# Node rows of a partition side by side: storing zu in another order and mapping the source list to it

## What is computed

```python
# layer 0 (4 heads of 16)
ZU = einsum('nd,kdr->knr', x, U);  zs, zd = ZU[:, src], ZU[:, dst]
alpha = segment_softmax((zs * zd).sum(-1) / 4, dst)
agg = segment_sum(alpha[..., None] * zs, dst)
ssa = einsum('k,knr,kdr->nd', softmax(head_w), agg, U)
Z_half = 0.5 * x + 0.5 * ssa
L0 = relu(Z_half + 0.5 * ((Z_half - (Z_half @ Dmat.T) @ Dmat) @ Dmat) - 0.05)
x = layernorm(x + L0)
# layer 1
agg = segment_sum(x[src], dst) / max(count, 1)
x = layernorm(x + relu(agg @ W_l.T + b_l + x @ W_r.T) + x)
```

## Time and profile before

| what | us |
|---|---|
| median of 3 runs (4514.98 to 4522.93) | 4522.0 |
| the profiled execution's own time | 4529.45 |
| its span, first to last instruction | 4527.6 |
| GpSimd busy in it (3493 instructions) | 3300.4 (73%) |
| VectorE busy | 2281.5 (50%) |
| TensorE, ScalarE busy | 931.8, 785.6 |
| edges of layer 0, GpSimd's part | 165.5 to 2205.5 |
| node stage of layer 0 | 2236 to 2396 |
| edges of layer 1, GpSimd's part | 2404.4 to 4340.7 |

### The profile page before, as it was taken

The page is one execution under the profiler, slowest core; times in us unless marked ns, Lnnn a source line. Parts: engine busy times, 40 slices in busy tenths (PEclk is TensorE's granted clock), DMA queues, the critical chain, the costliest instruction groups (busy, mean ns, idle before and its releaser), DMA issues. The chain is left out here.

```text
span 4527.6 us, 46280 instructions
## 1 busy us (share of the span) xinstructions
PE 931.8 (21%) x3091; PEld 613.9 (14%) x3091; DVE 2281.5 (50%) x9502; ACT 785.6 (17%) x1441; POOL 3300.4 (73%) x3493
## 2 busy tenths in 40 slices
PE   7301112111112000000293221122222221112027
PEld 7301101001001000000151110011111111001025
DVE  2107656666566666566473444344344344334348
ACT  2001101001001000000052222222222222222125
POOL 6677777777777777777565777777777777777755
PEclk6555555556556555555585555555555555555569
DMA  9803243333333322224284656666666666666769
GB/s 349 316 27 123 87 132 97 97 122 97 98 122 96 109 81 89 81 81 138 70 269 161 223 206 213 241 240 241 240 228 214 229 213 207 219 240 232 256 219 322
DMA packets 347584, 795.44 MB, mean 176 GB/s; under 512 B 94902, under 2 KB 235419, under 8 KB 317796
## 3 DMA queue, kind: packets, MB, share of 16 engines
q1 hardware_dynamic: 164706, 380.87, 23.6%
q0 software_dynamic: 137712, 276.64, 20.2%
q10 hardware_dynamic: 44818, 135.00, 7.7%
HBM read 420.40 MB, written 371.83 MB: 175 GB/s over the span
## 5 line engine op out<-in xcount | busy, mean ns | idle before, releaser
L575 POOL DMA_INDIRECT sb_big<-x,sb_idx x1549 | 1464.6, 946 | 502.8 <-issue 471.8
L575 POOL DMA_INDIRECT sb_big<-zu_rows,sb_idx x1531 | 1445.2, 944 | 478.4 <-issue 466.3
L1466 DVE SCALAR_TENSOR_TENSOR ps_V<-ps_V,sb_keepc,sb_big 128x256 f32<-128x256 f32 x1518 | 747.6, 493 | 132.7 <-ACT sb_big L1053 79.4
L1053 ACT COPY sb_big<-ps_V 128x1024 f32<-128x1024 f32 (+1 forms) x414 | 399.5, 966 | 1288.2 <-DVE ps_V L1466 1285.3
L762 PE MATMUL ps_T<-sb_ident,sb_xg 128*128 128x128 f32 x392 | 114.6, 390 | 2402.6 <-ACT sb_tileT L898 1225.0
L1466 DVE SCALAR_TENSOR_TENSOR ps_V<-ps_E,sb_keepc,sb_big 128x256 f32<-128x256 f32 x46 | 22.7, 492 | 1020.4 <-DMA sb_big<-x,sb_idx 981.0
L762 PEld LDWEIGHTS ps_T<-sb_ident,sb_xg 128*128 128x128 f32 x392 | 72.1, 201 | 2461.0 <-ACT sb_tileT L898 1236.2
L1272 DVE TENSOR_TENSOR_SCAN sb_big<-ps_E,sb_big 128x34 f32<-128x34 f32 x2944 | 355.3, 203 | 1.6
L1220 DVE TENSOR_TENSOR_SCAN ps_V<-ps_V,sb_big 128x34 f32<-128x34 f32 x2944 | 354.6, 206 | 0.0
L1229 DVE TENSOR_TENSOR sb_big<-ps_V,sb_big 128x2176 f32<-128x2176 f32 x46 | 111.4, 2421 | 351.3 <-DMA sb_big<-zu_rows,sb_idx 351.3
L575 POOL DMA_INDIRECT sb_hn<-rows,sb_nidx x196 | 189.5, 967 | 75.3 <-issue 53.6
(11 more groups left out here) (240 smaller groups left out, 1845.7 us busy)
## 6 DMA issues: line engine op xcount, KB each, us to landing
rows<-sb_big SPq DMA_DIRECT2D x46, 3072.0 KB, 10.7
rows<-sb_big SPq DMA_DIRECT2D x46, 1280.0 KB, 13.8
rows<-sb_big ACTq DMA_DIRECT2D x46, 1224.0 KB
z_at_start<-sb_big ACTq DMA_DIRECT2D x46, 1088.0 KB, 8.7
sb_big<-z_at_start SPq DMA_DIRECT2D x46, 1088.0 KB, 5.2
sb_zx<-zu_rows SPq DMA_DIRECT2D x2816, 0.2 KB
sb_big<-x SPq DMA_DIRECT2D x1920, 1.0 KB
sb_xg<-in_x_dram SPq DMA_DIRECT2D x36, 768.0 KB, 6.2
```

The lines of the kernel that those rows point to most:

```text
L575: pool.indirect_dma_start(to, None, table, bass.IndirectOffsetOnAxis(ap=index.bitcast(U32), axis=0), **more).then_inc(done, 16)
L1053: act.copy(slot1[s][:, cols, :], V0[:, first_word:first_word + width].rearrange("p (c f) -> p c f", f=D)).then_inc(col_copied, 1)
L1466: dve.scalar_tensor_tensor(out=sums_at(j), in0=before, scalar=keepc[:, j:j + 1], in1=slot1[s][:, j, :], op0=ALU.mult, op1=ALU.add).then_in ...
```

## The change

`zu_rows` gets another row order: within a group, the seven nodes of a partition stand side by side (row = 896 g + 7 p + b in place of 896 g + 128 b + p), so that each partition stores 1792 B in one piece. All other tables stay. Everything that reads `zu_rows` needs the new row numbers: VectorE maps `src_i` in place, and the one column for the carry row, with shifts and multiplications (six operations each, `rows_placed`); ScalarE waits for it before the first index copies. The offsets for layer 1 (`row_bytes[1]`) are made before the mapping. Between the layers VectorE maps `src_i` back in nine operations, with `normed` as working space, ahead of the scaling of group 0. The mapping uses the space of zs[0], so the zeros move to a piece of their own, half as long, which each fill reads twice. And GpSimd's queue changes its order: the gathers of chunk 1 now stand directly behind those of chunk 0, ahead of the scatters and the carry row.

```diff
@@ -79,9 +79,12 @@
     RB = 16
     U8 = mybir.dt.uint8
     NZ = 4
+    NTH, NTH_BITS = 147, 10
+    RTH, RTH_BITS = 9363, 16
     NX = 4
     assert FP * FQ == NF and FQ * FW <= C * F and CA % GC == 0 and NGC % 2 == 1 and C % GC == 2 and NG * GB == NB and NG % NX == 2 and NCH % 4 == 2 and NCH % S1 == 1 and NCH % 2 == 0 and NG < NCH // S1 and 0 < ELAST <= COLS and NF * FW == E
-    assert E <= EP and D == 2 * P
+    assert E <= EP and D == 2 * P and all(b * NTH >> NTH_BITS == b // GB for b in range(NB))
+    assert all(r * RTH >> RTH_BITS == r // GB for r in range(GN)) and GN * RTH < 1 << 24
 
     zu_rows = nc.dram_tensor("zu_rows", (NP, F), F32, kind="Internal").ap()
     z_at_start = nc.dram_tensor("z_at_start", (EP + NP, F), F32, kind="Internal").ap()
@@ -119,8 +122,8 @@
 
         regA = in_big(4 * C * F)
+        block_i = regA[:, 0:COLS].bitcast(I32)
         dst_i = regA[:, 2 * C * F:2 * C * F + COLS + 2].bitcast(I32)
-        zero = regA[:, C * F:2 * C * F]
         zs = [regA[:, s * C * F:(s + 1) * C * F].rearrange("p (c f) -> p c f", f=F) for s in range(2)]
         zd = [regA[:, (2 + s) * C * F:(3 + s) * C * F].rearrange("p (c f) -> p c f", f=F) for s in range(2)]
         zu = in_big(NB * F).rearrange("p (b f) -> p b f", f=F)
@@ -136,6 +139,7 @@
         Wraw = in_big(2 * KD * D).rearrange("p (w k n) -> p w k n", w=2, k=KD)
         Dm = in_big(KD * D).rearrange("p (k n) -> p k n", k=KD)
         DtD = in_big(KD * D).rearrange("p (k n) -> p k n", k=KD)
+        zero = in_big(C * F // 2)
 
         at_node = [0]
 
@@ -217,6 +221,8 @@
         zx_act = sb("zx_act", [P, F])
         nidx = [sb(f"nidx{s}", [P, GB], I32) for s in range(2)]
         zcar0 = sb("zcar0", [P, F])
+        zcar_i = sb("zcar_i", [P, 1], I32)
+        zcar_b = sb("zcar_b", [P, 1], I32)
         scar = sb("scar", [P, F + H])
         logit = sb("logit", [P, H, C])
         keepc = sb("keepc", [P, C])
@@ -271,7 +277,7 @@
         rows_counted = sem("rows_counted"); row_step = sem("row_step"); rows_known = sem("rows_known")
         found_rows = sems("found_rows", 2)
         first_known = sem("first_known"); next_made = sem("next_made"); nodes_known = sem("nodes_known"); z_scattered = sem("z_scattered")
-        zcar_loaded = sem("zcar_loaded")
+        zcar_loaded = sem("zcar_loaded"); rows_placed = sem("rows_placed")
         w_pe = sem("w_pe"); w_dve = sem("w_dve"); w_exp = sem("w_exp")
         idx_ready = sems("idx_ready", 2); zs_gathered = sems("zs_gathered", 2)
         zd_loaded = sems("zd_loaded", 2); zd_used = sems("zd_used", 2)
@@ -327,6 +333,10 @@
             return blocks(dram, g, 0, GB)
 
+        def side_by_side(dram, g):
+            return dram[bass.ds(g * GN, GN), :].rearrange("(p b) f -> p b f", p=P)
+
+
         def node_groups_of(engine, body):
 
             for u in range(NX):
@@ -388,7 +398,7 @@
 
             def store_zu(i, s):
                 sp.wait_ge(zu_copied, 2 * i + s + 1)
-                sp.dma_start(node_group(zu_rows, 2 * i + s), zu[:, bass.ds((2 * i + s) * GB, GB), :]
+                sp.dma_start(side_by_side(zu_rows, 2 * i + s), zu[:, bass.ds((2 * i + s) * GB, GB), :]
                              ).then_inc(zu_stored, 16)
 
             load_x(0, 0)
@@ -593,6 +603,7 @@
 
             pool.wait_ge(zu_stored, 16 * NG)
             gather_zs(0, 0, 0, 0)
+            gather_zs(0, 1, 0, 0)
 
             pool.wait_ge(nodes_known, 1)
             for q in range(NZ):
@@ -601,8 +612,8 @@
                 pool.indirect_dma_start(z_at_start, bass.IndirectOffsetOnAxis(ap=scat_i[:, b:b + 1].bitcast(U32), axis=0),
                                         zu[:, b, :], None).then_inc(z_scattered, 16)
 
-            gather(zcar0[:, :], zu_rows, dst_i[:, 1:2], zcar_loaded)
-            gather_zs(0, 1, 0, 0)
+            pool.wait_ge(rows_placed, 2)
+            gather(zcar0[:, :], zu_rows, zcar_i[:, 0:1], zcar_loaded)
 
             def later_rounds(i, pair, odd):
                 if isinstance(i, int) and i == 0:
@@ -863,7 +874,8 @@
             def fill(k, q):
 
                 wait(act, zero_filled[q], 16 * k)
-                act.dma_start(z_flat[:, bass.ds((NZ * k + q) * C * F, C * F)], zero).then_inc(zero_filled[q], 16)
+                act.dma_start(z_flat[:, bass.ds((NZ * k + q) * C * F, C * F)].rearrange("p (a f) -> p a f", a=2),
+                              zero.unsqueeze(1).broadcast_to([P, 2, C * F // 2])).then_inc(zero_filled[q], 16)
 
             act.wait_ge(zero_set, 1)
 
@@ -882,7 +894,7 @@
                              B[s][:, 0:GB * F].rearrange("p (b f) -> p b f", f=F)).then_inc(zu_copied, 1)
 
             rounds(act, NG // 2, project)
-            act.wait_ge(edges_loaded, 16 * 6)
+            act.wait_ge(rows_placed, 2)
             for s in range(2):
                 act.copy(idx[s][:, :], src_i[:, s * C:(s + 1) * C]).then_inc(idx_ready[s], 1)
             for k in range(NG // 2, -(-NCH // NZ)):
@@ -1111,6 +1123,23 @@
             dve.wait_ge(edge_ends, 32)
             dve.tensor_tensor(keep[:, :], dst_i[:, 1:COLS + 1], dst_i[:, 0:COLS], ALU.is_equal)
             dve.tensor_copy(ends, col_i)
+
+            for k, step, width in ((1, S1, D),):
+                last_cols = src_i[:, 0:NCH // step * step * C].rearrange("p (i c) -> p i c", c=step * C)[:, :, 2 * C - 1]
+                dve.tensor_scalar(row_bytes[k][:, :], last_cols, float(4 * width), None, ALU.mult
+                                  ).then_inc(rows_scaled, 1)
+            dve.wait_ge(rows_scaled, 1)
+
+            for row, blk, node_of in ((src_i[:, 0:COLS], block_i, src_i[:, 0:COLS]),
+                                      (zcar_i[:, :], zcar_b[:, :], dst_i[:, 1:2])):
+                done(dve.tensor_scalar(blk, node_of, P.bit_length() - 1, None, ALU.logical_shift_right))
+                done(dve.tensor_scalar(row, node_of, P - 1, None, ALU.bitwise_and))
+                done(dve.scalar_tensor_tensor(out=row, in0=row, scalar=float(GB), in1=blk, op0=ALU.mult, op1=ALU.add))
+                done(dve.tensor_scalar(blk, blk, float(NTH), None, ALU.mult))
+                done(dve.tensor_scalar(blk, blk, NTH_BITS, None, ALU.logical_shift_right))
+                dve.scalar_tensor_tensor(out=row, in0=blk, scalar=float(GN - GB), in1=row, op0=ALU.mult, op1=ALU.add
+                                         ).then_inc(rows_placed, 1)
+            dve.wait_ge(rows_placed, 2)
             done(dve.tensor_tensor(same, dst_i[:, 1:COLS + 1], dst_i[:, 2:COLS + 2], ALU.is_equal))
             done(dve.scalar_tensor_tensor(out=ends, in0=same, scalar=OUT_OF_RANGE, in1=ends, op0=ALU.mult,
                                           op1=ALU.add))
@@ -1189,7 +1218,7 @@
                                              ).then_inc(w_dve, 1)
 
-            for k, step, width in ((0, 2, F), (1, S1, D)):
+            for k, step, width in ((0, 2, F),):
                 last_cols = src_i[:, 0:NCH // step * step * C].rearrange("p (i c) -> p i c", c=step * C)[:, :, 2 * C - 1]
                 dve.tensor_scalar(row_bytes[k][:, :], last_cols, float(4 * width), None, ALU.mult
                                   ).then_inc(rows_scaled, 1)
@@ -1427,6 +1456,19 @@
 
             first_indices(0)
+
+
+            nodes_of = src_i[:, 0:COLS]
+            high, low = (n.rearrange("p b f -> p (b f)")[:, 0:COLS].bitcast(I32) for n in normed)
+            done(dve.tensor_scalar(high, nodes_of, P.bit_length() - 1, None, ALU.logical_shift_right))
+            done(dve.tensor_scalar(high, high, float(NTH), None, ALU.mult))
+            done(dve.tensor_scalar(high, high, NTH_BITS, None, ALU.logical_shift_right))
+            done(dve.tensor_scalar(high, high, float(GN), None, ALU.mult))
+            done(dve.scalar_tensor_tensor(out=nodes_of, in0=high, scalar=-1.0, in1=nodes_of, op0=ALU.mult, op1=ALU.add))
+            done(dve.tensor_scalar(low, nodes_of, float(RTH), None, ALU.mult))
+            done(dve.tensor_scalar(low, low, RTH_BITS, None, ALU.logical_shift_right))
+            done(dve.scalar_tensor_tensor(out=nodes_of, in0=nodes_of, scalar=float(P), in1=high, op0=ALU.mult, op1=ALU.add))
+            done(dve.scalar_tensor_tensor(out=nodes_of, in0=low, scalar=float(1 - GN), in1=nodes_of, op0=ALU.mult, op1=ALU.add))
             scale(0, 0, 0)
 
             def node_step(t, u):
```

## The result

| what | before | after |
|---|---|---|
| median of six runs each, us (lowest to highest) | 4522.81 (4514.98 to 4530.56) | 4548.26 (4545.36 to 4557.42) |
| the profiled execution's own time, us | 4529.45 | 4545.36 |
| GpSimd's first gather of zu rows | 165.51 | 156.63 |
| first scatter | 208.20 | 242.08 |
| first gather of chunk 2 | 378.84 | 405.06 |

The kernel became slower: ratio 1.006, 95% interval 1.0047 to 1.0073. The forecast was 4551 us, slower, 4540 to 4561; it held.

A forecast was written before the change was run, and what follows sets the result against it. GpSimd's gathers of zu rows, 1.249 us each, were taken to set the pace. Stall +33.7, front -7.5 and middle +3 sum to +29.2 us: 4551 against the median, range 4540 to 4561.

The forecast's parts named there:

- (a): GpSimd's queue order: nothing left to cover the chain to ScalarE's index copy, a stall of 33.7 us ahead of chunk 2.
- (b): Store of zu side by side: lands sooner, gaining between nothing and 11.55 us of GpSimd's wait of 11.86.
- (c): Map ahead on VectorE: holds up GpSimd's lookups by 4 us, range 0 to 6; front with store gains 7.5.
- Rival 1: The stall stands but VectorE does not hold GpSimd up: +22 us, 4544; chance 0.15.
- the three slow lookups agree: GpSimd's first lookups, 2.43, 2.11 and 1.49 us in place of 0.94, taken to support VectorE's two-port modes excluding GpSimd.
- the scatter at 208.20 without a wait: Front: taken to show all fills of zeros landed by then; the new order asks for them some 35 us later.
- (d): Map back between the layers: gathers beside it start about 4 us late, partly absorbed; +3 us, range 0 to 5.
- rival 4: Node stage: the granted clock falls elsewhere, sparing 13 us (4538) or adding as many; chance 0.07.
- Rival 2: Store: pieces stay 256 B or land no sooner, GpSimd starts at 165.5 as before: +36.7 us, 4559; chance 0.08.
- Rival 3: Later rounds: SyncE becomes the pace-maker; a round 1 us longer costs 8 us, 4559; chance 0.07.
- Rival 5: Gathers from the new table are cheaper on GpSimd; 40 ns less each gives 61 us, 4490; chance 0.03.

The follow-up runs named there:

- order alone: Kernel before with chunk 1's gathers moved ahead and a separate, half-long piece of zeros; old table, no map: 4547.67 us, ratio 1.0056.
- finer fills, whole memset: Kernel before whose fills read the first half of the piece of zeros twice, memset left whole: 4515.59 us in one run.
- finer fills: Kernel before with a half-long piece of zeros that each fill reads twice, memset half as long: 4521.73 us against 4526.96, ratio 0.9993.
- 6 ahead, old table: Kernel before with 6 of chunk 1's gathers ahead of the scatters, 28 behind the carry row, separate half-long zeros, no maps: 4516.77 us, ratio 0.9977.
- order undone: Changed kernel with chunk 1's 34 gathers behind the carry row again: 4525.81 us against 4521.06, ratio 1.0008.
- 6 ahead: Changed kernel with 6 of chunk 1's 34 gathers ahead of the scatters, 28 behind the carry row: 4518.52 us against 4521.06, ratio 0.9991.
- after, again: Changed kernel profiled once more, unchanged: 4551.6 us.
- 20 ahead: Changed kernel with 20 of chunk 1's 34 gathers ahead of the scatters, 14 behind the carry row: 4546.88 us.
- before, again: Kernel before profiled once more, unchanged: 4551.47 us.
- store alone: Kernel before with only the store side by side, list unmapped so wrong rows are gathered: 4517.06 us in one run, beside 4516.06.
- both maps: Changed kernel without the mapping ahead and back, so wrong rows are gathered, with the same amount of work: 4543.87 us, ratio 1.0047.

## Why the prediction was right

*(a) The stall.* This term was right, with its mechanism: predicted 33.7 us, measured 405.06 - 368.96 = 36.10 from the carry row's start to the next gather, less its own 1.27, so 34.8 (35.12 idle, with the usual 0.3 in it; 34.86, 35.15 and 35.16 idle in three other profiles). From the carry row's start to the end of ScalarE's copy it took 34.96 us before and 35.22 after (368.96 to 403.96 + 0.22); another 0.88 us passed until the gather began, of which the forecast had counted nothing. That it isn't given back is shown by the end of the edges, +26.2 us, where chunk 2 already stood. The lead of ScalarE's copy in the even chunks fell to 6.8 us at its least (6 predicted).

*(b) and (c), the front.* The sum was right (−7.5 predicted, −8.88 measured), and both parts are seen. The wait of 11.86 us fell to the usual 0.30 and the map ahead lengthened the lookups by 4.4 us (4 predicted), which makes −7.2. The other −1.7 is nothing that the prediction counted: the first lookup began at 26.51 in place of 28.23. In profiles of kernels that have at most one part of the change it begins anywhere from 26.32 to 28.40, so this much may be luck. GpSimd's and then VectorE's timeline of the changed kernel, to be held against the earlier trace rows:

```profile
26.51 2.42 POOL L585 DMA_INDIRECT sb_hn<-in_dst_dram,sb_frow_i  x1 [19.47 <-DVE sb_frow_i L1120]
29.24 1.80 POOL L585 DMA_INDIRECT sb_hn<-in_dst_dram,sb_frow_i  x1 [0.30 <-issue]
31.35 2.53 POOL L585 DMA_INDIRECT sb_hn<-in_dst_dram,sb_frow_i  x1 [0.30 <-issue]
34.18 1.40 POOL L585 DMA_INDIRECT sb_hn<-in_dst_dram,sb_frow_i  x1 [0.30 <-issue]
35.88 1.52 POOL L585 DMA_INDIRECT sb_hn<-in_dst_dram,sb_frow_i  x1 [0.31 <-issue]
```

```profile
29.95 0.97 DVE L1136 TENSOR_SCALAR sb_src_i<-sb_src_i 128x1564 int32<-128x1564 int32 x1
30.96 1.79 DVE L1137 SCALAR_TENSOR_TENSOR sb_src_i<-sb_src_i,sb_big 128x1564 int32<-128x1564 int32 x1
32.78 0.97 DVE L1138 TENSOR_SCALAR sb_big<-sb_big 128x1564 int32<-128x1564 int32 x1
33.79 0.97 DVE L1139 TENSOR_SCALAR sb_big<-sb_big 128x1564 int32<-128x1564 int32 x1
34.80 1.79 DVE L1140 SCALAR_TENSOR_TENSOR sb_src_i<-sb_big,sb_src_i 128x1564 int32<-128x1564 int32 x1
```

Rival 1, that VectorE does not hold GpSimd up, is thereby out: without the maps the second to fifth lookup take 0.97, 1.36, 1.52 and 0.94 us in place of 1.80, 2.53, 1.40 and 1.52, the two longer ones beside the wide operations that stay, and the lookups as a whole are 5.3 us shorter (from 26.33 to 150.86). A lookup that began at 29.24 ended at 31.04, 0.12 us after the tensor_scalar of line 1136; one that began at 31.35 ended at 33.88, 0.13 after that of line 1138. The prediction's reading of the earlier trace rows, that each of the first three lookups ended 0.8 us after a wide operation, holds for the second and third; the first ended 0.13 us after the cast (30.66 against 30.53). Of the three only that one has a cast beside it; the other two stand beside operations with two operands alone, so that the prediction's "the three slow lookups agree", said of two-port modes, holds for one of them. They are taken up at the end.

What the prediction did not see is what the gain of the front depends on. It priced the store and the order as terms that add up. They don't: undone, the order leaves chunk 2 where it was, although the first gather still starts 9 us earlier. It read the scatter at 208.20 without a wait as fills that were out of the way; they had landed within some 2 us before it. The windows of before would have told (us, busy and count of PE, PEld, DVE, ACT, POOL; clock, DMA share, GB/s):

```profile
165.00:180.00 15.00, 1.18 (x4) 0.93 (x4) 6.27 (x17) 0.00 (x0) 11.14 (x12) 0.50 1.02 418
180.00:200.00 20.00, 8.63 (x28) 5.52 (x28) 6.77 (x31) 0.30 (x1) 15.12 (x17) 0.67 1.02 412
200.00:215.00 15.00, 0.00 (x0) 0.00 (x0) 0.00 (x0) 0.00 (x0) 11.34 (x13) 0.50 0.43 159
```

The DMA engines are full up to 200 us and then fall to 0.43; in steps of 2 us the share is 0.99 from 202, 0.71 from 204 and 0.18 from 206 to 208. So the front is bound by them, and in the six kernels with at most 6 gathers of chunk 1 ahead whose first gather came early, the scatters started at 205.1 to 209.9. In the changed kernel the fills are hidden by the gathers moved ahead, which is the one good thing that the move does; it needs 6 to 8 of them, not 34. And the prediction credited the new store with the whole of the earlier landing; in the kernel with the order alone, which has the old store and the finer fills, the first gather came at 159.4, 6 us early without it.

*(d) The map back.* The late gathers came as laid out, and 3 us reach TensorE, as predicted (+3); what is left of them at the end of the stage is only roughly settled. GpSimd's first five gathers between the layers:

```profile
2266.50 2.77 POOL L585 DMA_INDIRECT sb_hn<-rows,sb_nidx  x1 [2.08 <-DMA rows<-sb_scratch,sb_end_i]
2269.57 1.40 POOL L585 DMA_INDIRECT sb_hn<-rows,sb_nidx  x1 [0.30 <-issue]
2271.28 1.52 POOL L585 DMA_INDIRECT sb_hn<-rows,sb_nidx  x1 [0.30 <-issue]
2273.10 1.52 POOL L585 DMA_INDIRECT sb_hn<-rows,sb_nidx  x1 [0.30 <-issue]
2274.93 0.94 POOL L585 DMA_INDIRECT sb_hn<-rows,sb_nidx  x1 [0.31 <-issue]
```

The fifth starts 8.43 us after the first, 3.4 more than four times 1.249 us (4 predicted); the nine operations took 11.5 us (11.2 to 16.1 predicted) and fit into VectorE's idle time. TensorE's warm-up hides the delay for the first two groups. The third group's first matmul shows it, TensorE's timeline before and then after:

```profile
2272.88 0.41 PE L809 MATMUL ps_T<-sb_ident,sb_big 128*64 128x128 f32 x2
```

```profile
2302.66 0.61 PE L820 MATMUL ps_T<-sb_ident,sb_big 128*64 128x128 f32 x2 [2.13 <-DVE sb_big L1403]
```

That is 33.2 us after the first gather between the layers before and 36.2 after. In all eight profiles without the map back it is 32.8 to 33.7 us and TensorE comes to it without a wait; in all five with it, 36.2 to 36.7 us, and TensorE has waited 2.1 to 3.3 us for VectorE's scaled rows. What reached the end of the stage can only be read at the same granted clock:

| kernel | node stage, us | clock |
|---|---|---|
| old list: finer fills, whole memset | 151.58 | 0.95 |
| old list: finer fills | 150.37 | 0.93 |
| map back: after | 153.58 | 0.93 |
| old list: 6 ahead, old table | 159.43 | 0.85 |
| map back: order undone; 6 ahead; after, again | 161.90; 162.20; 160.86 | 0.85 |
| old list: before | 164.64 | 0.82 |
| map back: 20 ahead | 166.87 | 0.82 |
| old list: before, again; order alone; store alone | 151.97; 153.37; 155.35 | 0.90 |
| left out: both maps | 155.29 | 0.90 |

At equal clock the stage with the map back is 3.2, 1.4 to 2.8, and 2.2 us longer; three stages of one and the same form without it at 0.90 lie 3.4 us apart, so the mean clock fixes the length no better than that. And the rows answer rival 4: the clock moves the stage by up to 14 us, but as much between two executions of one kernel (before 164.64 and 151.97; after 153.58 and 160.86) as between kernels. So it is why the two first profiles are only 15.9 us apart, and it can scatter the medians. Whether the change has no part in it is not shown, though: right behind TensorE's wait at the third group the granted clock was 0.50 over the next 14 us in four of the five profiles with the map back (0.89 in the first profile of the changed kernel), and 1.00 in all eight without it. In six of those eight it fell later, to 0.50 to 0.57, for one to three groups of some 14.5 us in place of 8.1. The mean stage is 161.1 us with the map back (five profiles) and 155.3 without (eight). Such a cost would come on top of the 3 us; these few profiles don't settle it, and the medians, with 25.4 us against the 27 to 29 of the sum, give no sign of it.

*The other rivals.* Rival 2, a store that lands no sooner, is out for the side-by-side form (5.6 and 5.7 us in the two kernels that show it, against 8.3 at the least); that the old store alone scatters between 8 and 55 us wasn't among the cases. Rival 3, SyncE as pace-maker, didn't come: after 405.06 GpSimd waits once for 0.3 us. Rival 5, cheaper gathers, is out: 944 ns.

So the sum of +29.2 us in the prediction is made in these profiles of +34.8 for the stall, −8.9 for the front and +1.4 to +3.2 for the middle, 27 to 29; the medians moved by 25.4 us, whose interval in the ratio (0.47 to 0.73%) is 21 to 33 us.

## What to carry over

Before work is moved forward in a queue, ask what it covered where it was: 34 gathers of 1.25 us hid a chain of 35 us, and moving only as many as the new gap takes (6, the old table kept) turned a loss of 25 us into a gain of 5 to 16 over the kernel before (0.11 to 0.35%). An engine that starts without a wait right when a transfer ends is no evidence of slack; the DMA share of the windows around it is. And two repairs of the same front don't add up where a third thing, here the fills, ends just behind them.

## What the hardware showed that I had not expected

**A store held up beside the fills.** In the second profile of the kernel before, the stores' line reads (ns min/median/max, first and last start; then its landing):

```profile
L391 SPq DMA_DIRECT2D zu_rows<-sb_big x14: 381/397/12015, 31.6 to 144.3; - x14
...
DMA to landing us min/median/max: 7.3/11.3/54.3
```

The same for the changed kernel:

```profile
L401 SPq DMA_DIRECT2D zu_rows<-sb_big x14: 340/356/602, 29.5 to 148.4; - x14
...
DMA to landing us min/median/max: 4.6/6.5/13.6
```

In 256 B pieces even the issue of a store took up to 12.0 us and its landing up to 54.3; in 1792 B pieces 0.6 and 13.6, for the same bytes. Over all profiles the longest issue is 5.7 to 12.0 us in the six with 256 B pieces and 0.4 to 1.6 in the seven with 1792 B. The longest landing tells less: in the kernel with the order alone, in 256 B pieces, it is 13.7. The window of that second profile, 165 to 180 us, had the DMA engines at a share of 1.02 with GpSimd doing nothing:

```profile
165.00:180.00 15.00, 1.17 (x4) 0.93 (x4) 6.72 (x18) 0.00 (x0) 0.00 (x0) 0.50 1.02 411
```

The fills went first, as it seems: the share is 1.02 to 0.98 up to 200, where the last store lands (199.42), and 0.16 from there to 215, against 0.43. The Trainium skill ("DMA: Bandwidth & Descriptors", Queues, rings and completion order) has each DMA engine going round between its queues a packet at a time; small pieces would then get a small share of the bytes beside large ones. The longer issues and landings of the small pieces agree in direction; that the share of the bytes is the cause is an inference. A spread of 8 to 55 us for one and the same store is more than the rule explains. Whether such executions are the reason for the kernel before's slower runs (five of 23 on one chip took 4538 to 4541 us) was not shown. They would be what the side-by-side store is good for: no kernel with it showed a late store, in seven profiles. But one late store in six profiles with 256 B pieces can be chance, and the four of these whose fills read in halves show none either.

**What of a VectorE operation holds a GpSimd gather.** The rows of the front above fit one reading. A wide operation that is under way when a gather begins, be it a cast or one with one or two operands, holds the gather's start; the gather then ends 0.81 or 0.82 us behind it (34.18 + 1.40 = 35.58 against 33.79 + 0.97 = 34.76; 35.88 + 1.52 = 37.40 against 34.80 + 1.79 = 36.59). If a one-operand operation or a cast is under way when the gather would end, it is held once more and ends 0.12 or 0.13 us behind that one (31.04 and 33.88 above). A two-operand one did not hold the end: the gather that ended at 35.58 had line 1140's beside it, from 34.80 to 36.59. A tensor_reduce did not hold at all (0.94 us for the gather at 42.37, beside line 1146's), nor did, in the kernel without maps, a tensor_tensor that began only 0.04 us before the gather (0.97 us). The Trainium skill ("SBUF — State Buffer", Who interferes with whom) says that two inputs in SBUF contend only with GpSimd's reads, which agrees, and that tensor_tensor did not stall a DMA from there, which doesn't: these rows show a gather of 2.53 us, in place of 0.94, that ends 0.81 us after a tensor_tensor with both operands in SBUF.

```profile
37.71 2.53 POOL L585 DMA_INDIRECT sb_hn<-in_dst_dram,sb_frow_i  x1 [0.30 <-issue]
...
37.64 1.79 DVE L1143 TENSOR_TENSOR sb_big<-sb_big 128x1564 f32<-128x1564 int32 x1
```
